# A decoder matmul over pairs of row blocks: eight half-size products become seven

## The chip, the core and the metric

The kernel runs on one core of one Trainium2 chip. The time is the device time of one execution in microseconds (us), the median of three runs. The engines are TensorE (PE in the profile, its weight loads PEld), VectorE (DVE), ScalarE (ACT), GpSimd (POOL) and the DMA queues, here that of SyncE (SP).

## What is computed

Two layers of a graph network with a normalization ahead of each, on 1250 nodes of 1024 features, 20000 edges. With `h = relu(layernorm(x))`, the first layer is

```python
h = jax.nn.sigmoid(x @ wenc.T + benc)
h2 = h @ conv_weight
msgs = h2[src] * edge_weight[:, None]
agg = jax.ops.segment_sum(msgs, dst, num_segments=x.shape[0])
hout = agg + h @ lin_weight.T
p = hout @ wdec.T + bdec
```

with 500 features inside, and `x + p` goes on. The decoder is the last line: a 1250x500 by 500x1024 product. The second layer is `x + D (A + I) D (relu(layernorm(x)) W.T + b)` with the degree scaling `D`. All of it is float32. The kernel gets float32 accuracy out of TensorE by writing each operand as a high part (rounded to fp32r or f16) and a low part, the rest; a product is then three passes: high by high, high by low, low by high.

## The kernel before

Rows come in ten blocks of 125 (`PB`), which pair up in five groups `g` of 250 (`GN`). The 500 inner features are four blocks `fo` or `j` of 125. Each engine has its own program, written out in the order in which it runs; `wait_ge` and `then_inc` on semaphores (class `Signal`) are the only ties between them. An engine does nothing ahead of an instruction that waits.

The stages in order: encoder and a count of edges into dense matrices (to about 128 us), aggregation (three steps of `AGG`; step 2, with groups 3 and 4, is the last), decoder (`decode`), second norm (`norm2_...`), the product U with the adjacency matrix (`u_group`), and the product with W (`w_product`, itself done as seven half-size products over pairs of row blocks).

**Aggregation to decoder.** ScalarE (`agg_evac`) copies each aggregated block out of PSUM as `ouhi`, VectorE subtracts to get `oulo`. The decoder weight `wd32` comes in by one 2 MB DMA, ScalarE rounds it to `wdhi`, VectorE makes `wdlo`, a quarter after each block of step 2.

**Decoder.** For each row block `k` and column half `c` TensorE does 4 feature blocks by 3 passes, 12 matmuls with 512 columns, into one of six PSUM banks (`dec_bank`): 20 tiles, 240 matmuls. A tile waits until the tile six before it has been read.

**Second norm.** For each tile VectorE adds the bank to `x1` (`residual`, the tensor that the profile shows as x) and takes its statistics; for each row block it then aggregates, ScalarE takes a root, and VectorE makes scale and bias in seven small steps (`norm2_step`) between the adds of the next block. ScalarE (`norm2_apply`) writes `ghi` (f16, 1024 wide) and two halves `t32`, a ring of four buffers; GpSimd subtracts to get `glo`, for the last block VectorE does.

**After it.** `u_group` asks for six banks at once ahead of its first matmul, 2 to 7 (`bank_of`), then goes through the row blocks `d`, twelve matmuls for each, and needs `ghi[d]` and `glo[d]`. When the last `glo` is made, SyncE loads W, and `x1` plus a bias is written away to DRAM; ScalarE's and VectorE's preparation of W (`W_hi`, `W_lo`) and GpSimd's row sums follow on that.

Of the kernel before, what the change touches and what calls it, by code (L numbers as in the profile page):

```python
# [113 lines left out]
def build(nc, x, src, dst, ew, dst_s, sd_rows, w_rows, wenc, benc, conv, lin, wdec, W, b, out):  # L114
# [331 lines left out]
    wdhi_ok = signal("wdhi_ok", one(FB))  # L446
    wdlo_ok = signal("wdlo_ok", one(FB))
# [3 lines left out]
    dec_done = signal("dec_done", KC)  # L451
    x1_ok = signal("x1_ok", KC)
    ve_ok = signal("ve_ok", one(NB))
    sqk_ok = signal("sqk_ok", one(NB))
    nb2_ok = signal("nb2_ok", one(NB))
# [1480 lines left out]
```

## Time and profile before

| | us |
|---|---|
| median of three runs | 470.31 (470.27 to 470.35) |
| profiled execution | 470.15 |
| its span in the trace | 468.3 |
| decoder on TensorE | 227.43 to 283.24 |
| TensorE busy in the span | 462.2 (99%) |
| VectorE, ScalarE, GpSimd busy | 286.6, 196.7, 109.9 |

Times inside the trace count from the start of the span. The profiled execution has 1.85 us outside its span. A busy TensorE says that a matmul was in flight; how fast they follow each other is read from the start times. Where a row of the timeline has a part in brackets, the engine stood idle before it and the bracket says for what.

### The profile page before, as it was taken

How to read it: one execution, taken by the hardware profiler on the slowest of the kernel's cores; microseconds unless marked ns; L12 is line 12 of the kernel's file. 1: busy time of each engine (PE TensorE's matmuls, PEld its weight loads, DVE VectorE, ACT ScalarE, POOL GpSimd, SP SyncE). 2: the span in 40 equal slices, each digit the busy share in tenths (PEclk: the TensorE clock that was granted, in tenths of full speed). 3: DMA queues.
4: the chain of work that ended last, by engine and by line, in shares of the span. 5: the costliest groups of instructions: out<-in, count | busy, mean ns of one | idle time of the engine just before them, and what ended most of it. 6: DMA issues, size and time to landing. Idle time of an engine off the chain costs nothing.

```text
span 468.3 us, 7228 instructions
## 1 busy us (share of the span) xinstructions
PE 462.2 (99%) x3158; PEld 369.6 (79%) x2658; DVE 286.6 (61%) x531; ACT 196.7 (42%) x371; POOL 109.9 (23%) x104
## 2 busy tenths in 40 slices
PE   8999999999999999999999999999999999999997
PEld 6999999988888899888877775444449878787876
DVE  7999878898576398022367885994130095344443
ACT  6897975855485104022024446024442512221210
POOL 2500000000040000000013443000003599895640
PEclk9999999999999999999999999999999999999999
DMA  8720004000000237100499600833310133613113
GB/s 297 272 91 2 1 2 176 2 1 1 2 1 2 83 121 247 53 0 1 173 323 174 102 1 1 316 151 131 133 69 1 57 131 145 227 55 89 44 45 91
DMA packets 26315, 44.69 MB, mean 95 GB/s; under 512 B 15525, under 2 KB 15836, under 8 KB 25638
## 3 DMA queue, kind: packets, MB, share of 16 engines
q1 hardware_dynamic: 26024, 43.77, 29.2%
q8 instruction: 25, 0.41, 0.4%
q0 software_dynamic: 224, 0.39, 0.3%
q14 instruction: 12, 0.10, 0.1%
q10 hardware_dynamic: 30, 0.02, 0.0%
HBM read 27.53 MB, written 13.41 MB: 87 GB/s over the span
## 4 chain that ended last, share of the span: by engine, by line
PE 90%; ACT 4%; DVE 4%; issue 1%; POOL 0%; POOLq 0%; DVEq 0%
PE ps L1446 87%; PE ps L1450 3%; ACT junk L718 1%; ACT zhi L747 1%; PE ps L1464 1%; ACT xn L740 1%; ACT wehi L734 1%; ACT wide L723 0%; DVE h_all L1040 0%; DVE zlo L1028 0%; ACT wide L729 0%; ACT h L756 0%; ACT h_all L759 0%; DVE h_all L1116 0%; DVE m_hot L1064 0%
## 5 line engine op out<-in xcount | busy, mean ns | idle before, releaser
L1446 PE MATMUL ps<-CT,ghi 125*128 125x500 f16 (+1 forms) x240 | 77.0, 339 | 0.0
L1446 PE MATMUL ps<-CT,glo 125*128 125x500 f16 (+1 forms) x240 | 76.9, 339 | 0.0
L1429 DVE SCALAR_TENSOR_TENSOR x1b<-ps,dsc,x1b 125x512 f32<-125x512 f32 x49 | 35.1, 746 | 34.3 <-PE ps L1446 34.2
L661 POOL TENSOR_TENSOR glo<-t,ghi 125x512 f16<-125x512 f32 x18 | 20.6, 1164 | 136.6 <-ACT t L888 136.6
L673 POOL TENSOR_TENSOR S<-U_all 128x500 f32<-128x500 f32 x25 | 31.6, 1273 | 83.8 <-DVE Blo L1403 58.6
L1446 PE MATMUL ps<-A_lo,h2hi 125*125 125x500 f32 (+1 forms) x120 | 42.3, 353 | 0.0
L1446 PE MATMUL ps<-wdhi,h_all 125*125 125x512 f32 (+1 forms) x128 | 40.3, 395 | 0.0
L1446 PE MATMUL ps<-zhi,wehi 128*125 128x250 f32 x160 | 39.3, 288 | 0.2
L1446 PE MATMUL ps<-Bhi,Shi 128*125 128x512 f32 (+1 forms) x144 | 39.3, 388 | 0.0
L1446 PE MATMUL ps<-Blo,Shi 128*125 128x512 f32 (+1 forms) x144 | 39.3, 388 | 0.0
L1446 PEld LDWEIGHTS ps<-CT,ghi 125*128 125x128 f16 x240 | 23.5, 98 | 19.0 <-issue 0.3
L1446 PEld LDWEIGHTS ps<-CT,glo 125*128 125x128 f16 x240 | 23.5, 98 | 18.8
L1446 PE MATMUL ps<-zlo,wehi 128*125 128x250 f32 x160 | 36.8, 279 | 0.0
L1446 PE MATMUL ps<-zhi,welo 128*125 128x250 f32 x160 | 36.1, 279 | 0.0
L925 ACT ACTIVATE Shi<-S 128x500 fp32r<-128x500 f32 x25 | 15.5, 622 | 47.9 <-POOL S L673 29.0
L681 POOL TENSOR_TENSOR Slo<-S,Shi 128x500 fp32r<-128x500 f32 x25 | 33.7, 1349 | 0.0
L1446 PEld LDWEIGHTS ps<-Blo,Shi 128*125 128x125 f32 x144 | 26.7, 185 | 6.4
L1446 PEld LDWEIGHTS ps<-Bhi,Shi 128*125 128x125 f32 x144 | 26.6, 185 | 6.3
L1446 PE MATMUL ps<-Ahi,h2lo 125*125 125x500 f32 x80 | 31.3, 391 | 0.0
L1446 PE MATMUL ps<-Ahi,h2hi 125*125 125x500 f32 x80 | 31.2, 390 | 0.0
L767 ACT ACTIVATE C<-ps 125x250 f16<-125x250 f32 x50 | 19.9, 398 | 26.2 <-PE ps L1450 26.1
L1446 PEld LDWEIGHTS ps<-wdhi,h_all 125*125 125x125 f32 (+1 forms) x128 | 23.8, 186 | 6.0
(181 smaller groups left out, 1032.0 us busy)
## 6 DMA issues: line engine op xcount, KB each, us to landing
xn<-in_x_dram SPq DMA_DIRECT2D x10, 512.0 KB, 5.9
x<-in_x_dram SPq DMA_DIRECT2D x10, 512.0 KB
x_scratch<-x SPq DMA_DIRECT2D x10, 500.0 KB
x1b<-x_scratch SPq DMA_DIRECT2D x10, 500.0 KB
out_dram<-x1b SPq DMA_DIRECT2D x19, 240.0 KB
B<-in_W_dram SPq DMA_DIRECT2D x4, 1024.0 KB, 8.0
c_scratch<-C SPq DMA_DIRECT2D x10, 305.2 KB
wd<-in_wdec_dram SPq DMA_DIRECT2D x1, 2048.0 KB, 15.6
```

Of the source, the lines that this page charges most:

```text
L661: p.tensor_tensor(glo[k][0:PB, cs], t32[(2 * k + c) % 4][0:PB, :], ghi[k][0:PB, cs], ALU.subtract).then_inc(*glo_p.up(k, c))
L673: p.tensor_tensor(S32[m][:, :, :], quarter(u, *one_of), quarter(u, *other), op).then_inc(*S_ok.up(u, m))
L681: p.tensor_tensor(o_ap, of, f32(Shi[W_SEQ.index((u, m)) % 6][:, :, :]), ALU.subtract).then_inc(*Slo_ok.up(u, m))
L718: a.activation(junk[0:HW], ps_all[0:HW, 0:5, 0:500], ACT.Sign, scale=-1.0, bias=thr_half[0:HW, i:i + 1], accum_out=cnt[0:HW, i:i + 1]).the ...
L734: a.activation(wehi[f][:, 0:k1, :], we32[f][:, 0:k1, :], ACT.Copy).then_inc(*whi_a.up(f, 0))
L740: a.activation(part, part, ACT.Relu, **kw).then_inc(*relu_a.up(k, h))
L747: a.activation(zhi[g % 2][:, 4 * h:4 * h + 4, i * PB:i * PB + PB], ps[turn_bank(k, h)][:, 0:4 * PB].rearrange("p (k n) -> p k n", n=PB), A ...
L767: a.activation(C[0:PB, :, u * 25:u * 25 + 25].rearrange("p a (w l) -> p a w l", w=WD), v[:, 0], ACT.Copy)
L925: a.activation(Shi[n % 6][:, :, :], of, ACT.Copy).then_inc(*Shi_ok.up(u, m))
L1429: v.scalar_tensor_tensor(r, ps[bank8["w", u, m]][0:PB, 0:512], scale, r, ALU.mult, ALU.add).then_inc(*term_ok.up(u, m, n))
L1446: return t.matmul(o_ap, lhsT, rhs, start=start, stop=stop)
L1450: return t.add_instruction(mybir.InstMatmult(name=nc.get_next_instruction_name(), engine=mybir.EngineType.PE, ins=[t.lower_ap(rhs), t.lowe ...
```

## The change

The decoder's product for a pair of row blocks is a 2 by 2 block product: two row blocks, two halves of the inner features, two halves of the columns. It was done as eight half-size products (each 2 feature blocks by 3 passes). Now it is done as seven, numbered 1 to 7, on sums and differences of blocks: `op_sums` makes four sums of the activations of a group on GpSimd (`oS`), `wd_sum` makes four sums of the weight there (`D32`), and the results of the products are added up as follows, with x11 the left half of the first row block:

- x11 += P1, P2; V = P1 + P6; V5 = V + P5; x12 += P3 + V5; x21 += V + P7 + P4; x22 += V5 + P7, where the sign of a product is in its weight's sum.

ScalarE copies P1 into `V` (`keep_product`). VectorE makes V and V5 and adds every product to `x1`, eight instructions for a pair in place of four. GpSimd adds V to x21 and V5 to x12 and x22 (`side_add`). A product takes one bank, in a ring of all eight. The activations are evacuated whole (`ou`), and high and low parts are made of blocks and sums by ScalarE (`op_hi`) and VectorE or, for groups 3 and 4, GpSimd (`op_lo`). The second norm goes by pairs. `t32` has three buffers. Four memsets at the start of VectorE's program go, since the row of ones for the bias now lies in `ohi` and GpSimd writes it.

```diff
-    wdlo = at("wdlo", RA, [128, FB, DIM], F32R)
-    wdhi = [at(f"wdhi_{j}", o, [128, DIM], F32R) for j, o in enumerate(
-        [RA + 16384 + j * 4096 for j in range(3)] + [RH + 4 * H_SLOT])]
...
+    ou = [at(f"ou_{g}", RH + g * H_SLOT, [128, FB, GN], F32) for g in range(NG)]
+    oulo = [at(f"oulo_{g}", RH + g * H_SLOT, [128, FB, GN], F32R) for g in range(NG)]
+    oS = [at(f"oS_{g}", RH + g * H_SLOT + 4000, [128, 4, 2, PB], F32) for g in range(NG)]
+    oSlo = [at(f"oSlo_{g}", RH + g * H_SLOT + 4000, [128, 4, 2, PB], F32R) for g in range(NG)]
+    ohi = [at(f"ohi_{g}", RG + g * 8192, [128, 7, 2, PB], F32R) for g in range(NG)]
+    V = [at(f"V_{i}", RA + 40960 + i * 2048, [128, 512], F32) for i in range(2)]
+    V5 = [at(f"V5_{i}", RA + 45056 + i * 2048, [128, 512], F32) for i in range(2)]
...
-    t32 = [at(f"t32_{i}", t32o[i], [128, 512], F32) for i in range(4)]
+    t32 = [at(f"t32_{i}", RH + i * 2048, [128, 512], F32) for i in range(3)]
...
+    D_ORDER = (1, 6, 2, 5, 3, 7, 4)
+    D_OP = {1: 0, 2: 1, 4: 2, 5: 3, 6: 4, 7: 5, 3: 6}
+    D_BANKS = (7, 0, 1, 6, 2, 3, 4, 5)
+    D_READ = {1: "x11a", 6: "V", 2: "x11b", 5: "V5", 3: "x12", 7: "x22", 4: "x21b"}
...
+        def op_sums(g):
+            A11, A12, A21, A22 = (ou[g][0:PB, 2 * j:2 * j + 2, i * PB:i * PB + PB] for i in range(2) for j in range(2))
+            S1, S2, S3, S4 = (oS[g][0:PB, i] for i in range(4))
+            p.wait_ge(*ou_ok.at(g, FB - 1))
+            p.tensor_tensor(S1, A21, A22, ALU.add).then_inc(*ps_step.up())
+            first = ps_step.now()
+            p.tensor_tensor(S3, A11, A21, ALU.subtract)
+            p.wait_ge(*first)
+            p.tensor_tensor(S2, S1, A11, ALU.subtract).then_inc(*ps_step.up())
+            p.wait_ge(*ps_step.now())
+            p.tensor_tensor(S4, A12, S2, ALU.subtract).then_inc(*oS_ok.up(g))
...
+        op_sums(0)
+        op_sums(1)
+        p.wait_ge(*agg_done.at(1, FB - 1))
+        op_ones(0)
+        p.wait_ge(*d_wd.at())
+        B11, B12, B21, B22 = (wd32[:, i] for i in range(4))
+        wd_sum(7, B22, B12)
+        p.wait_ge(*dsum_ok.at(7))
+        wd_sum(5, B12, B11)
+        p.wait_ge(*dsum_ok.at(5))
+        wd_sum(6, B22, D32[5])
+        p.wait_ge(*dsum_ok.at(6))
+        wd_sum(4, B21, D32[6])
+        op_sums(2)
+        p.wait_ge(*agg_done.at(2, 0))
+        op_ones(1)
+        op_ones(2)
+        p.wait_ge(*agg_done.at(2, FB - 1))
+        op_ones(3)
+        op_ones(4)
+        wd_lo(5)
+        def side_add(g, what, of, after):
+            k, c = 2 * g + int(what[1]) - 1, int(what[2]) - 1
+            r = x1[0:PB, k, 512 * c:512 * c + 512]
+            p.wait_ge(*add_ok.at(g, after))
+            if what == "x21":
+                p.wait_ge(*d_x1[k].at("x"))
+            p.tensor_tensor(r, r, of[g % 2][0:PB, :], ALU.add).then_inc(*side_ok.up(g, what))
+        for g in range(NG):
+            side_add(g, "x21", V, "V")
+            if g < 2:
+                op_sums(g + 3)
+            else:
+                gather_lo((0, 2, 4)[g - 2])
+            side_add(g, "x12", V5, "x12")
+            side_add(g, "x22", V5, "x22")
+            if g < 2:
+                for i in range(3):
+                    op_lo(g + 3, i)
+            elif g < NG - 1:
+                gather_lo((1, 3)[g - 2])
+        for k in range(5, NB - 1):
+            gather_lo(k)
...
+        def op_hi(g):
+            a.wait_ge(*ones_ok.at(g))
+            a.wait_ge(*oS_ok.at(g))
+            for i in range(3):
+                a.activation(op_high(g, i), op_of(g, i), ACT.Copy).then_inc(*ohi_ok.up(g, i))
+        def keep_product(g):
+            if g >= 2:
+                a.wait_ge(*side_ok.at(g - 2, "x21"))
+                a.wait_ge(*add_ok.at(g - 2, "V5"))
+            a.wait_ge(*dec_done.at(g, 1))
+            a.activation(V[g % 2][0:PB, :], ps[dec_bank(g, 1)][0:PB, 0:512], ACT.Copy).then_inc(*kept_ok.up(g))
...
+            if (step, fo) == (2, FB - 1):
+                a.wait_ge(*agg_done.at(step, fo))
+                wd_hi(5)
+                wd_hi(3)
+                keep_product(0)
+                wd_hi(7)
+                wd_hi(4)
...
+        op_hi(3)
+        keep_product(1)
+        for g in range(NG):
+            norm2_root(g)
+            if g == 0:
+                op_hi(4)
+            norm2_apply(2 * g)
+            if g + 2 < NG:
+                keep_product(g + 2)
+            norm2_apply(2 * g + 1)
...
-        for g in range(NG - 1):
-            v.memset(f32(hhi[g][:, 0, :]), 1.0).then_inc(*one_row.up(g))
...
+        def norm2_step(g, n):
+            ks = slice(2 * g, 2 * g + 2)
+            each = [slice(k, k + 1) for k in range(2 * g, 2 * g + 2)]
+            y, t, s2, var, dg = (col[name] for name in ("ry", "rt", "sc2", "ve", "nb"))
             if n == 0:
-                v.wait_ge(*sqk_ok.at(k))
-                v.reciprocal(y, col["sq"][0:PB, ks]).then_inc(*vs.up())
+                v.wait_ge(*sqk_ok.at(g))
+                v.reciprocal(y[0:PB, ks], col["sq"][0:PB, ks]).then_inc(*vs.up())
             else:
                 v.wait_ge(*step_done[0])
             if n == 1:
-                v.tensor_tensor(t, y, y, ALU.mult).then_inc(*vs.up())
+                for k in each:
+                    v.tensor_scalar(t[0:PB, k], y[0:PB, k], var[0:PB, k], y[0:PB, k], ALU.mult, ALU.mult).then_inc(*vs.up())
             if n == 2:
-                v.tensor_tensor(t2, t, var, ALU.mult).then_inc(*vs.up())
+                v.tensor_scalar(t[0:PB, ks], t[0:PB, ks], -0.5, 1.5, ALU.mult, ALU.add).then_inc(*vs.up())
             if n == 3:
-                v.tensor_scalar(t, t2, -0.5, 1.5, ALU.mult, ALU.add).then_inc(*vs.up())
+                for k in each:
+                    v.tensor_scalar(s2[0:PB, k], t[0:PB, k], y[0:PB, k], dg[0:PB, k], ALU.mult, ALU.mult).then_inc(*vs.up())
             if n == 4:
-                v.tensor_tensor(r, t, y, ALU.mult).then_inc(*vs.up())
-            if n == 5:
-                v.tensor_scalar(s2, r, col["dinv"][0:PB, ks], GSCALE, ALU.mult, ALU.mult).then_inc(*vs.up())
-            if n == 6:
-                v.scalar_tensor_tensor(col["nb2"][0:PB, ks], mv[0:PB, k, 0:1], -1.0, s2, ALU.mult, ALU.mult
-                                       ).then_inc(*nb2_ok.up(k))
+                for i, k in enumerate(each):
+                    ins = v.tensor_scalar(col["nb2"][0:PB, k], mv[0:PB, 2 * g + i, 0:1], s2[0:PB, k], -1.0, ALU.mult, ALU.mult)
+                ins.then_inc(*nb2_ok.up(g))
             step_done[0] = vs.now()
...
+        for g in range(NG):
+            if g == 0:
+                wd_lo(3)
+            else:
+                norm2_stats(g - 1, 1, 0)
+                norm2_stats(g - 1, 0, 1)
+            shared_sum(g)
+            add_product(g, 1, "x11a")
+            add_product(g, 2, "x11b")
+            if g == 0:
+                wd_lo(7)
+            else:
+                norm2_stats(g - 1, 1, 1).then_inc(*vs.up())
+                step_done[0] = vs.now()
+            right_sum(g)
+            if g == 0:
+                wd_lo(4)
+            else:
+                norm2_var(g - 1)
+            norm2_stats(g, 0, 0)
+            add_product(g, 3, "x12")
+            for n in range(2 if g else 0):
+                norm2_step(g - 1, n)
+            add_product(g, 7, "x21a")
+            for n in range(2, 4 if g else 2):
+                norm2_step(g - 1, n)
+            add_product(g, 7, "x22")
+            for n in range(4, 5 if g else 4):
+                norm2_step(g - 1, n)
+            add_product(g, 4, "x21b")
...
+                    if n >= 8:
+                        g0, i0 = divmod(n - 8, 7)
+                        t.wait_ge(*add_ok.at(g0, D_READ[D_ORDER[i0]]))
+                    elif n == 0:
+                        t.wait_ge(*ou_ok.at(2, FB - 1))
+                    elif n in (4, 7):
+                        t.wait_ge(*ou_ok.at(NG - 1, FB - 2 if n == 4 else FB - 1))
+                    o_ap = ps[dec_bank(g, m)][0:PB, 0:512]
+                    op, i = D_OP[m], op_part(m)
+                    q0, i0 = (0 if op == 0 else 2), (PB if op == 2 else 0)
+                    t.wait_ge(*ohi_ok.at(g, i))
+                    if g == 0:
+                        t.wait_ge(*dhi_ok.at(m))
+                    for j in range(2):
+                        K = PB + 1 if m in (1, 5) and j == 0 else PB
+                        mm(o_ap, ohi[g][0:K, op, j, :], Dhi[m][0:K, j, :], j == 0, False)
+                    t.wait_ge(*(olo_v if g < 3 else olo_p).at(g, i))
+                    for j in range(2):
+                        L = oulo[g][0:PB, q0 + j, i0:i0 + PB] if op < 3 else oSlo[g][0:PB, op - 3, j, :]
+                        mm(o_ap, L, Dhi[m][0:PB, j, :], False, False)
+                    if g == 0:
+                        t.wait_ge(*(dlo_v if (m,) in dlo_v.values else dlo_p).at(m))
+                    for j in range(2):
+                        K = PB + 1 if m in (1, 5) and j == 0 else PB
+                        ins = mm(o_ap, ohi[g][0:K, op, j, :], Dlo[m][0:K, j, :], False, j == 1)
+                    ins.then_inc(*dec_done.up(g, m))
...
-                if bank < 6:
-                    t.wait_ge(*x1_ok.at(*KC[18 + bank if bank < 2 else 12 + bank]))
+                g0, i0 = divmod(max(n for n in range(7 * NG) if D_BANKS[n % 8] == bank), 7)
+                t.wait_ge(*add_ok.at(g0, D_READ[D_ORDER[i0]]))
```

**VectorE, one pair of row blocks in the decoder, before** (second norm of one block `k`, done twice for a pair; x_156 is `x1`, rt, sc_68 and nb_69 are small columns):

```order
L1328 TENSOR_TENSOR x_156<-x_156,ps 125x512
L1340 RECIPROCAL ry<-sq 125x1
L1328 TENSOR_TENSOR x_156<-x_156,ps 125x512
L1344 TENSOR_TENSOR rt<-ry 125x1
L1332 BN_STATS stats<-x_156 125x6
L1346 TENSOR_TENSOR rt_65<-rt,ve 125x1
L1332 BN_STATS stats<-x_156 125x6
L1348 TENSOR_SCALAR rt<-rt_65 125x1
L1350 TENSOR_TENSOR rstd<-rt,ry 125x1
L1352 TENSOR_SCALAR sc_68<-rstd,dinv 125x1
L1354 SCALAR_TENSOR_TENSOR nb_69<-mv,sc_68 125x1
L1375 BN_AGGR mv<-stats 125x2
```

**and after** (one pair; x_195 is `x1`, V_173 is V, V_0_175 is V5):

```order
L1492 TENSOR_TENSOR V_173<-V_173,ps 125x512
L1486 TENSOR_TENSOR x_195<-x_195,ps 125x512 x2
L1508 BN_STATS stats<-x_195 125x6
L1501 TENSOR_TENSOR V_0_175<-V_173,ps 125x512
L1512 BN_AGGR mv<-stats 125x2
L1513 BN_AGGR mv<-stats 125x2
L1128 TENSOR_SCALAR ve<-mv 125x2
L1508 BN_STATS stats<-x_195 125x6
L1486 TENSOR_TENSOR x_195<-x_195,ps 125x512
L1524 RECIPROCAL ry<-sq 125x2
L1529 TENSOR_SCALAR rt<-ry,ve 125x1 x2
L1486 TENSOR_TENSOR x_195<-x_195,ps 125x512
```

The four adds and four statistics of a pair have become eight adds or sums and four statistics, and the small instructions run once for a pair on two columns or two after each other.

**ScalarE, from the end of the aggregation to the second pair's norm, after** (ohi are the high parts of a group's activations, V_173 and V_174 the kept products, ghi and t the norm's outputs):

```order
L964 ACTIVATE ohi_171<-ou_151 125x500
L964 ACTIVATE ohi_171<-ou_151 125x250
L964 ACTIVATE ohi_171<-oS_161 125x1000
L972 ACTIVATE V_174<-ps 125x512
L1019 ACTIVATE sq<-ve 125x2
L964 ACTIVATE ohi_172<-ou_152 125x500
L964 ACTIVATE ohi_172<-ou_152 125x250
L964 ACTIVATE ohi_172<-oS_162 125x1000
L1024 ACTIVATE ghi_196<-x_195,nb_69,sc_68 125x1024
L1029 ACTIVATE t_0_217<-x_195,nb_69,sc_68 125x512
L1029 ACTIVATE t_1_218<-x_195,nb_69,sc_68 125x512
L972 ACTIVATE V_173<-ps 125x512
```

The copies of product 1 (L972) stand in the row with the norm's writes; before, nothing but roots and those writes stood here.

**GpSimd, over the same stretch, after** (L698 to L704 are the sums of a group, L756 the side adds, L712 low parts):

```order
L719 TENSOR_TENSOR Dlo_182<-wd_177,Dhi_191 126x1024
L756 TENSOR_TENSOR x_195<-x_195,V_173 125x512
L698 TENSOR_TENSOR oS_161<-ou_151 125x250
L700 TENSOR_TENSOR oS_161<-ou_151 125x250
L702 TENSOR_TENSOR oS_161<-oS_161,ou_151 125x250
L704 TENSOR_TENSOR oS_161<-ou_151,oS_161 125x250
L756 TENSOR_TENSOR x_195<-x_195,V_0_175 125x512 x2
L712 TENSOR_TENSOR oulo_156<-ou_151,ohi_171 125x4x125
L712 TENSOR_TENSOR oulo_156<-ou_151,ohi_171 125x2x125
L712 TENSOR_TENSOR oSlo_166<-oS_161,ohi_171 125x1000
L756 TENSOR_TENSOR x_195<-x_195,V_174 125x512
L698 TENSOR_TENSOR oS_162<-ou_152 125x250
```

Before, only the subtractions for `glo` stood here. The sums and low parts of groups 3 and 4 now stand between the side adds of groups 0 and 1.

## Rows read from the trace of the kernel before

**Rows 1.** the page: busy time, share of the span, instructions; then the chain

```profile
PE 462.2 (99%) x3158; PEld 369.6 (79%) x2658; DVE 286.6 (61%) x531; ACT 196.7 (42%) x371; POOL 109.9 (23%) x104
...
PE 90%; ACT 4%; DVE 4%; issue 1%; POOL 0%; POOLq 0%; DVEq 0%
```

**Rows 2.** the busy time by stretch: decoder, then U's first half

```profile
core 0: us, PE busy (x) PEld busy (x) DVE busy (x) ACT busy (x) POOL busy (x), PEclk, DMA share, GB/s
...
227.40:283.20 55.80, 55.80 (x241) 44.37 (x239) 39.92 (x116) 21.51 (x34) 16.05 (x14) 1.00 0.73 162
...
283.20:317.00 33.80, 33.80 (x162) 15.68 (x162) 29.76 (x36) 9.87 (x16) 4.54 (x4) 1.00 0.42 165
```

**Rows 3.** TensorE's timeline: start, duration (us), matmul (decoder begins, U begins)

```profile
227.43 0.39 PE L1446 MATMUL ps<-wdhi,ouhi 126*125 126x512 f32 x1
...
283.24 0.38 PE L1446 MATMUL ps<-CT,ghi 125*128 125x500 f16 x1
```

**Rows 4.** VectorE's timeline in the decoder

```profile
241.78 0.69 DVE L1328 TENSOR_TENSOR x<-x,ps 125x512 f32<-125x512 f32 x1
...
242.39 0.15 DVE L1340 RECIPROCAL ry<-sq 125x1 f32<-125x1 f32 x1
...
247.45 0.16 DVE L1354 SCALAR_TENSOR_TENSOR nb<-mv,sc 125x1 f32<-125x1 f32 x1
...
247.53 0.20 DVE L1375 BATCH_NORM_AGGREGATE mv<-stats 125x2 f32<-125x12 f32 x1
...
247.76 0.15 DVE L982 TENSOR_SCALAR ve<-mv 125x1 f32<-125x1 f32 x1
```

**Rows 5.** groups of instructions: count, busy us, mean ns of one, idle before

```profile
L1296 DVE TENSOR_TENSOR wdlo<-wd,wdhi 128x1024 fp32r<-128x1024 f32 x4 | 4.8, 1224 | 0.6 <-ACT wdhi L876 0.6
...
L884 ACT ACTIVATE ghi<-x,nb,sc 125x1024 f16<-125x1024 f32 x10 | 12.3, 1227 | 0.0
...
L888 ACT ACTIVATE t<-x,nb,sc 125x512 f32<-125x512 f32 x20 | 15.1, 802 | 0.0
...
L925 ACT ACTIVATE Shi<-S 128x500 fp32r<-128x500 f32 x25 | 15.5, 622 | 47.9 <-POOL S L673 29.0
...
L876 ACT ACTIVATE wdhi<-wd 128x1024 fp32r<-128x1024 f32 x4 | 4.1, 1060 | 0.0
...
L661 POOL TENSOR_TENSOR glo<-t,ghi 125x512 f16<-125x512 f32 x18 | 20.6, 1164 | 136.6 <-ACT t L888 136.6
...
L673 POOL TENSOR_TENSOR S<-U_all 128x500 f32<-128x500 f32 x25 | 31.6, 1273 | 83.8 <-DVE Blo L1403 58.6
...
L681 POOL TENSOR_TENSOR Slo<-S,Shi 128x500 fp32r<-128x500 f32 x25 | 33.7, 1349 | 0.0
```

**Rows 6.** the timeline where VectorE and GpSimd want SBUF together

```profile
249.98 0.69 DVE L1328 TENSOR_TENSOR x<-x,ps 125x512 f32<-125x512 f32 x1 [1.37 <-PE ps L1446]
...
250.08 2.29 POOL L661 TENSOR_TENSOR glo<-t,ghi 125x512 f16<-125x512 f32 x2 [3.77 <-ACT t L888]
...
251.79 0.60 DVE L1346 TENSOR_TENSOR rt<-rt,ve 125x1 f32<-125x1 f32 x1
...
17.13 0.99 POOL L625 DMA_INDIRECT sdw<-in_sd_rows_dram,row_i  x1 [0.30 <-issue]
...
17.75 0.35 DVE L1000 TENSOR_SCALAR ry<-ve 125x2 int32<-125x2 int32 x1
```

**Rows 7.** the page's DMA issues: KB, us to landing

```profile
wd<-in_wdec_dram SPq DMA_DIRECT2D x1, 2048.0 KB, 15.6
```

**Rows 8.** VectorE's timeline at the start: the four memsets

```profile
2.16 1.07 DVE L1116 MEMSET h_all<- 128x250 f32 x4
```

**Rows 9.** the timeline behind the decoder: VectorE, GpSimd and TensorE

```profile
293.77 12.04 DVE L1393 SCALAR_TENSOR_TENSOR x<-bb,vb,x 125x1024 f32<-125x1024 f32 x10
...
350.84 2.46 POOL L673 TENSOR_TENSOR S<-U_all 128x500 f32<-128x500 f32 x2 [58.60 <-DVE Blo L1403]
...
367.70 1.16 PE L1446 MATMUL ps<-Bhi,Shi 128*125 128x512 f32 x4
```

More of the change, by code:

```diff
@@ L437, in build @@
     OU_PARTS = [(g, fo) for gs in AGGS for fo in range(FB) for g in gs]
-    ouhi_ok = signal("ouhi_ok", OU_PARTS)
-    oulo_ok = signal("oulo_ok", OU_PARTS)
+    ou_ok = signal("ou_ok", OU_PARTS)
+    oS_ok = signal("oS_ok", one(NG))
+    ones_ok = signal("ones_ok", one(NG))
+    OP_PARTS = [(g, i) for g in range(NG) for i in range(3)]
+    ohi_ok = signal("ohi_ok", OP_PARTS)
+    olo_v = signal("olo_v", OP_PARTS[:9])
+    olo_p = signal("olo_p", OP_PARTS[9:])
+    ps_step = Steps(sem("pool_step"))
     deg_a = signal("deg_a", [(k,) for k in range(0, NB, 2)])
@@ L445, in build @@
     va_ok = signal("va_ok", one(NB))
[L446 to L455, printed above, removed]
+    dsum_ok = signal("dsum_ok", [(7,), (5,), (6,), (4,)])
+    dhi_ok = signal("dhi_ok", [(1,), (2,), (6,), (5,), (3,), (7,), (4,)])
+    dlo_v = signal("dlo_v", [(1,), (2,), (6,), (3,), (7,), (4,)])
+    dlo_p = signal("dlo_p", [(5,)])
+    GM = [(g, m) for g in range(NG) for m in D_ORDER]
+    dec_done = signal("dec_done", GM)
+    add_ok = signal("add_ok", [(g, what) for g in range(NG) for what in ("V", "x11a", "x11b", "V5", "x12", "x21a", "x22", "x21b")])
+    kept_ok = signal("kept_ok", one(NG))
+    side_ok = signal("side_ok", [(g, what) for g in range(NG) for what in ("x21", "x12", "x22")])
+    ve_ok = signal("ve_ok", one(NG))
+    sqk_ok = signal("sqk_ok", one(NG))
+    nb2_ok = signal("nb2_ok", one(NG))
     ghi_ok = signal("ghi_ok", one(NB))
@@ L1280, in vector @@
         for step, fo, groups, parts in AGG:
-            for n in groups:
-                agg_evac(n, fo)
             for part in parts:
                 split_A(*part)
+            if (step, fo) == (1, FB - 1):
+                v.wait_ge(*dsum_ok.at(5))
+                wd_lo(1)
+                v.wait_ge(*dsum_ok.at(4))
+                wd_lo(2)
+                op_lo(0)
+            if step == 2 and fo < 2:
+                if fo == 0:
+                    wd_lo(6)
+                op_lo(fo + 1)
             if step == 0:
@@ new lines, in norm2_stats, with norm2_var @@
+        def norm2_stats(g, half, c):
+            k = 2 * g + half
+            v.wait_ge(*{(0, 0): add_ok.at(g, "x11b"), (1, 0): add_ok.at(g, "x21b"), (0, 1): side_ok.at(g, "x12"),
+                        (1, 1): side_ok.at(g, "x22")}[half, c])
+            return v.bn_stats(stats[0:PB, k, c, :], x1[0:PB, k, 512 * c:512 * c + 512])
+        def norm2_var(g):
+            v.wait_ge(*step_done[0])
+            v.bn_aggr(mv[0:PB, 2 * g, :], stats[0:PB, 2 * g].rearrange("p a s -> p (a s)"))
+            v.bn_aggr(mv[0:PB, 2 * g + 1, :], stats[0:PB, 2 * g + 1].rearrange("p a s -> p (a s)")).then_inc(*vs.up())
+            v.wait_ge(*vs.now())
+            with_eps(2 * g, 2 * g + 2).then_inc(*ve_ok.up(g))
@@ L1378, in vector, with late_stats @@
-        for n in range(7):
-            norm2_step(NB - 1, n)
+        def late_stats(g):
+            norm2_stats(g, 1, 0)
+            norm2_stats(g, 0, 1)
+            norm2_stats(g, 1, 1).then_inc(*vs.up())
+            step_done[0] = vs.now()
[10 more added lines that the diff above has]
+                wd_lo(7)
+            else:
+                norm2_stats(g - 1, 1, 1).then_inc(*vs.up())
+                step_done[0] = vs.now()
+            right_sum(g)
+            if g == 0:
+                wd_lo(4)
+            else:
+                norm2_var(g - 1)
[10 more added lines that the diff above has]
+            add_product(g, 4, "x21b")
@@ L1380, in vector @@
+        late_stats(NG - 1)
+        norm2_var(NG - 1)
+        for n in range(5):
+            norm2_step(NG - 1, n)
         k = NB - 1
```

190 lines of the change are left out of this document (95 added, 95 removed).

## The prediction

> **What bounds the kernel now.** First the page's busy line and its chain [rows 1]: TensorE is busy 99% of the span and the chain that ended last is 90% TensorE, so a microsecond of matmuls taken out is a microsecond won, unless a wait takes its place. Then the stages [rows 2]: in the decoder and in U after it TensorE never stops, at a granted clock of 1.00 (2.4 GHz), while VectorE is busy 39.9 of 55.8 us, ScalarE 21.5, GpSimd 16.1. Those three get the new work. Then TensorE's start times [rows 3]: 240 matmuls from 227.43 to 283.24 are 55.81 us, 0.2325 us each (the duration of 0.39 overlaps the next one).
>
> **TensorE's part.** 7 products x 5 groups x 6 matmuls = 210, of the same 512 columns and the same three passes. 30 fewer x 0.2325 = **6.98 us less**; a group takes 42 x 0.2325 = 9.77 us in place of 11.16, all five 48.8, and the decoder could end at 276.3. Nothing is added on TensorE.
>
> **Prices for the rest.** VectorE starts the instruction behind a 512-wide add 0.61 us later (241.78 to 242.39 [rows 4]); small ones follow each other in 0.08 us when independent and 0.23 when one waits for the other (247.45, 247.53, 247.76 [rows 4]). The two-pointer `tensor_scalar` of the new norm has no row; between 0.08 and 0.25 I take 0.13, since they come in independent pairs. A 1024-wide subtraction on VectorE is 1.22, taken as 1.17 back to back [rows 5]. ScalarE [rows 5], less 0.1 us that neighbours overlap: `ghi` 1.13, a `t` 0.71, a copy of 500 elements 0.52, of 250 half of that and a little, 0.28, of 1024 0.96. The copy of product 1 has the size of the 500-element one, about 0.60 to its end. GpSimd: 1.16 to 1.35 us for 500 to 512 elements [rows 5], 1.23 apart in the two at 350.84 [rows 9], so 1.25 for a side add, 1.14 for half a `glo`, about 0.65 for 250 elements, 2.4 for 1000. A handover between engines is 0.05 to 0.15.
>
> **The port.** A VectorE instruction with two SBUF inputs that needs 0.14 lasts 0.60 while GpSimd works (251.79 plus 0.60 is 252.39, GpSimd ends at 252.37 [rows 6]): it waits until GpSimd's instruction is over. An add from PSUM keeps its 0.69 beside GpSimd (249.98 [rows 6]). A two-column `tensor_scalar` lasts 0.35, where small ones take 0.15 to 0.20 [rows 4], and ends as GpSimd's descriptor write does, at 18.1 [rows 6].
>
> **What the edits cost ahead of the decoder.** The weight's and activations' sums and the high and low parts for groups 0 to 2 are covered by TensorE's step 2, 168 matmuls of 500 columns or some 38 us, in which the other engines mostly wait for it. The weight lands 15.6 us after its issue [rows 7]; even if that were issued only as step 2 starts, GpSimd's four weight sums, 9.6 us, and one group's, 2.6 us, would end 10 us ahead of the decoder. So they cost nothing; without that cover they would cost those 12 us. At 227.45 it gets tight. ScalarE rounds weight 5 (to 228.5), GpSimd makes its low part, 2.4 us, to 231.0, and VectorE, which wanted weight 3 at 229.5, is held off the port until then: V(0) is done at 232.9. Weights 7 and 4 come just late for TensorE, together about 0.6 us, so its own end is **276.9**.
>
> **The chain through V.** Three things stand in a row that before had nothing to do with each other. Product 1 must be copied by ScalarE before VectorE can make V; ScalarE's copy for group g+2 stands behind `norm2_apply(2g)`; that waits for the norm of group g, whose last small step VectorE takes near the end of its work for group g+1.
>
> Start of it: GpSimd's side add ends at 234.1. VectorE's low parts of weights 7 and 4 take the port (1.17 each) between the sums of group 3, which end at 239.1. Two side adds to 241.6; low parts of group 3, 1.23 + 0.62 + 2.40, to 245.8; side add to 247.1; sums of group 4, 4 x 0.65 and 0.2 of port, to 249.9. ScalarE's high parts of group 4, 0.52 + 0.28 + 0.95, stand ahead of the first norm writes: 251.7; `ghi` and two `t`, 1.13 + 1.42: 254.2; the copy and handover: **V(2) starts at 254.9**. TensorE had product 6 of group 2 ready at about 250.5.
>
> A lap, V(g) to V(g+1): on VectorE nine wide instructions (V, two adds, statistics, V5, statistics, three adds) 9 x 0.61 = 5.5; one of them waits for its neighbour, 0.1; small ones 1.6 (2 aggregates and epsilon 0.41, reciprocal 0.19, three pairs 0.78, one of two columns 0.18): 7.2, with 0.1 for the root that is late once. On ScalarE handover 0.1, `ghi` 1.13, `t` 0.71, a wait of 0.35 (the ring has three buffers, and the one needed is freed by GpSimd only after the side add of x22, 1.25, and half a `glo`, 1.14), `t` 0.71, copy and handover 0.65: 3.65. Together 10.95, and about 0.25 for the two-column step held by the port: **11.2 us, where TensorE needs 9.77**.
>
> Two laps: V(4) starts at 277.3. TensorE does not feel it inside the decoder, since eight banks let it run seven products (9.8 us) ahead. It feels it at the end: U asks for banks 2 to 7 before its first matmul, and bank 7 holds the last group's product 3, whose add (x12) VectorE starts 5 x 0.61 + 0.1 + 0.4 + 0.61 = 4.2 us after V(4), at 281.5, and ends at 282.2. So TensorE stands from 276.9 to 282.3, **5.4 us**, and U begins at 282.3 in place of 283.24. Of 6.98 us, 0.9 are left.
>
> **The rest.** The four memsets, 1.07 us [rows 8], leave VectorE's start. Behind them stands the cast that TensorE and ScalarE wait for, so between 0 and 1.07; VectorE then waits for the x rows' DMA anyway, so I take 0.2. After the decoder: the last `glo`, made 16 us after x12 (rest of the adds and statistics, norm steps, then ScalarE's six writes, paced by GpSimd's halves of 1.14), comes at about 298.4, and VectorE's bias (293.77 [rows 9]), the loads of W and GpSimd's first sums (350.84 [rows 9]) move some 4.6 us later, to 355.5; these sums and their low parts take 4.9 us, to 360.4, and TensorE wants them at 367.7 [rows 9] less 1.1. Covered, and covered for `glo[d]` too: U takes 2.5 us for a block. Sum: 470.15 of the profiled execution less 0.9 less 0.2 = 469.05; the median lies 0.16 above that execution, so **469.2**.
>
> **A rule against the trace.** The row of the held instruction and the row of the two-column one [rows 6] are all that this trace shows of the port. The Trainium skill ("SBUF — State Buffer", section "SBUF: two separate sides") says that VectorE's two-input instructions and those in a two-port mode share one exclusive port pair with GpSimd, for the whole instruction. The trace agrees for two inputs. By that rule the epsilon step (two columns, one input) would be held as well, which is rival B: 471.0 where the sum above has 469.2.
>
> **Rivals.**
> - A, the lag stays small. If GpSimd's 250-wide sums and the pairs on VectorE are quicker, V(2) starts at 252.5 and the lap is 10.5 without port and ring waits: x12 at 277.7 to 278.4, U at 278.5, gain 4.7, 465.4; if the lap is below 9.8 the change does all it says, 463.3. For it: the port waits are short where GpSimd idles. Against: the order of ScalarE's program is fixed, and nine adds of 0.61 are measured. 463 to 468, chance 0.20.
> - B, slower: small steps held by the port. GpSimd works 5 x 1.2 us of each lap, so each held step costs up to 1.25. With epsilon held too a lap is 12.1: V(4) 279.1, U at 284.1, 471.0. With all pairs held a lap is 13.1: U at 286.1, 473.0. The point from which the change loses: lap = 11.2 + 0.95 / 2 = 11.7. Chance 0.20.
> - C, slower: the clock. TensorE is idle 5.4 us in one piece, longer than any gap in this trace, where the granted clock is 1.00 [rows 2]. If it drops to 1.2 GHz for as long as the gap was, U's matmuls go at half rate for 5.4 us: 2.7 lost, 471.9. The Trainium skill ("TensorE: Matmul & The Clock Gate", section "Part 1: The HAM clock gate (the "warmup" mystery)") says that idleness throttles the array to that level; no row here shows it. Chance 0.15.
> - The forecast, U between 280.8 and 283.8, 467.7 to 470.8: 0.40. Something else, mostly at the start or in the W stage: 0.05.
>
> **How the numbers follow.** The range leaves out the best tenth (below 466.0, most of A's lower half) and the tail of B: 466.0 to 473.0. A measurement of this kernel tells 0.2% (0.94 us) from no change, so faster ends at 469.4. Faster: 0.27 of the forecast's 0.40, all of A, 0.01 of the rest: 0.48. Same (to 471.25): 0.12 + 0.08 of B + 0.02 of C + 0.02: 0.24. Slower: 0.01 + 0.12 + 0.13 + 0.02: 0.28.
>
> **What would show it.** TensorE without a gap in the decoder but with one of 4 to 6 us between its last matmul and the first of U, put down to VectorE's add into x (L1486). V's adds (L1492) near 254.9, 266.1 and 277.3. VectorE idle before each of them for ScalarE's copy (L972). I am wrong if that gap is under 3 us or the V's are less than 10.5 apart (A), if the two-column steps last over 0.5 (B), or if the granted clock of the first 10 us of U is under 0.9 (C).

## The result, and the profile after

The changed kernel takes 472.18 us (median of five, 471.38 to 472.87), the kernel before 470.28 (470.27 to 470.35) in the same comparison: ratio 1.0041, 95% interval 1.0029 to 1.0052. It is slower by 1.9 us, where 469.2 was forecast. The profiled execution took 472.11 and has a span of 470.1.

TensorE's busy line, the clock by fortieths of the span, and the chain, from the page of the changed kernel (of before: [rows 1]):

```profile
PE 458.6 (98%) x3128; PEld 365.0 (78%) x2628; DVE 296.4 (63%) x504; ACT 210.9 (45%) x389; POOL 172.2 (37%) x159
PEclk9999999999999999999999997999999999999999
PE 85%; DVE 6%; POOL 3%; issue 3%; ACT 2%; DMA 1%; DVEq 0%; POOLq 0%; ACTq 0%
```

Thirty matmuls are gone, the chain's share on TensorE fell from 90% to 85%, and one slice of the clock, the 25th (282 to 294 us), is not full. TensorE's longest wait behind 46 us (engine, line, what for: us in all, times, longest; the only other, 0.4 us, lies ahead of the decoder), and its timeline around the decoder's end:

```profile
PE ps L1649 <- DVE x L1486: 5.8, 1, 5.8
```

```profile
276.18 0.63 PE L1649 MATMUL ps<-Dlo,ohi 125*125 125x512 f32 x2
282.64 0.58 PE L1649 MATMUL ps<-CT,ghi 125*128 125x500 f16 x1 [5.83 <-DVE x L1486]
283.01 0.62 PE L1649 MATMUL ps<-CT,glo 125*128 125x500 f16 x1
283.42 0.63 PE L1649 MATMUL ps<-CT,ghi 125*128 125x500 f16 x1
...
287.18 0.51 PE L1649 MATMUL ps<-CT,glo 125*128 125x500 f16 x1
287.52 0.38 PE L1649 MATMUL ps<-CT,ghi 125*128 125x500 f16 x1
287.73 0.37 PE L1649 MATMUL ps<-CT,glo 125*128 125x500 f16 x1
```

The decoder is over at 276.65 (276.18 and two starts of 0.2325), U begins at 282.64, where it was 283.24 [rows 3]: one wait, for the add of the last group's product 3 (x12). The profile calls it 5.8 us; counted from the slot in which the next matmul would have started it is 6.0. Then U's first twelve matmuls start 0.42 us apart, the later ones 0.211. The same by stretch (start:end, us, TensorE busy, granted clock, DMA share, GB/s):

```profile
276.00:282.60 6.60, 0.81 (x4) 0.85 0.00 0
282.60:287.60 5.00, 4.96 (x13) 0.52 0.02 5
287.60:292.60 5.00, 5.00 (x26) 1.00 0.00 0
```

After the wait the granted clock is 0.52, the level of 1.2 GHz, and TensorE, busy all the time, gets 13 matmuls into 5 us in place of 26. The level fell inside the wait already, where the mean is 0.85. From 282.64 to 287.52 there are twelve matmuls, 4.88 us; at 0.211 they would be 2.53. That is **2.35 us lost**, and the whole account is: start of the decoder 227.14 for 227.43, 0.3 less; 30 matmuls, 7.0 less; waits inside the decoder, 0.7 more; the wait at its end, 6.0 more; the clock, 2.35 more. Sum +1.8, as the span says (470.1 less 468.3).

What the wait hangs on, on VectorE, ScalarE and GpSimd (V of groups 2, 3 and 4, and what is ahead of them):

```profile
253.92 0.69 DVE L1492 TENSOR_TENSOR V<-V,ps 125x512 f32<-125x512 f32 x1 [3.03 <-ACT V L972]
257.34 0.17 DVE L1128 TENSOR_SCALAR ve<-mv 125x2 f32<-125x2 f32 x1
265.05 0.69 DVE L1492 TENSOR_TENSOR V<-V,ps 125x512 f32<-125x512 f32 x1 [1.71 <-ACT V L972]
268.47 0.92 DVE L1128 TENSOR_SCALAR ve<-mv 125x2 f32<-125x2 f32 x1
272.97 0.33 DVE L1537 TENSOR_SCALAR nb<-mv,sc 125x1 f32<-125x1 f32 x2
276.92 0.69 DVE L1492 TENSOR_TENSOR V<-V,ps 125x512 f32<-125x512 f32 x1 [1.71 <-ACT V L972]
280.35 0.86 DVE L1128 TENSOR_SCALAR ve<-mv 125x2 f32<-125x2 f32 x1
281.72 0.66 DVE L1486 TENSOR_TENSOR x<-x,ps 125x512 f32<-125x512 f32 x1
```

```profile
273.33 1.24 ACT L1024 ACTIVATE ghi<-x,nb,sc 125x1024 f16<-125x1024 f32 x1 [3.71 <-DVE nb L1537]
274.48 0.80 ACT L1029 ACTIVATE t<-x,nb,sc 125x512 f32<-125x512 f32 x1
275.59 0.82 ACT L1029 ACTIVATE t<-x,nb,sc 125x512 f32<-125x512 f32 x1 [0.31 <-POOL glo L725]
276.31 0.57 ACT L972 ACTIVATE V<-ps 125x512 f32<-125x512 f32 x1
```

```profile
267.07 2.28 POOL L725 TENSOR_TENSOR glo<-t,ghi 125x512 f16<-125x512 f32 x2
278.91 2.27 POOL L725 TENSOR_TENSOR glo<-t,ghi 125x512 f16<-125x512 f32 x2
```

The rows read as a loop: VectorE's last norm step of group 2 (272.97) lets ScalarE write `ghi` and two `t`, only then comes the copy of product 1 of group 4 (276.31), and VectorE, idle for 1.71 us, starts V(4) at 276.92. A lap, from one V to the next, is 11.13 and then 11.87 us. In the second the epsilon step of two columns (it adds the norm's small constant to the variances of two row blocks) takes 0.92 and ends at 269.39, when GpSimd's pair does (269.35); the same at 280.35, on the way to x12.

### The profile page after: what moved, and what is told of

Read it like the earlier page. It is cut to its first block, busy times and chain, and to the rows that moved or that the text cites. A ratio compares the mean times of both kernels' runs of the same rounds, so it can differ in the third digit from the quotient of the medians.

```text
span 470.1 us, 7278 instructions
## 1 busy us (share of the span) xinstructions
PE 458.6 (98%) x3128; PEld 365.0 (78%) x2628; DVE 296.4 (63%) x504; ACT 210.9 (45%) x389; POOL 172.2 (37%) x159
## 4 chain that ended last, share of the span: by engine, by line
PE 85%; DVE 6%; POOL 3%; issue 3%; ACT 2%; DMA 1%; DVEq 0%; POOLq 0%; ACTq 0%
PE ps L1649 80%; PE ps L1653 3%; DVE x L1486 2%; PE ps L1667 1%; POOL x L756 1%; DVE stats L1508 1%; DMA xn<-in_x_dram 1%; ACT ohi L964 1%; POOL wehi L671 1%; DVE V L1501 1%; POOL glo L725 0%; ACT V L972 0%; DVE xn L1270 0%; POOL oS L698 0%; POOL oS L700 0%
## 5 line engine op out<-in xcount | busy, mean ns | idle before, releaser
L1649 PE MATMUL ps<-CT,ghi 125*128 125x500 f16 (+1 forms) x240 | 78.4, 345 | 5.8 <-DVE x L1486 5.8
L1649 PE MATMUL ps<-CT,glo 125*128 125x500 f16 (+1 forms) x240 | 78.3, 345 | 0.0
L691 POOL TENSOR_TENSOR C<-C,loops 125x125 f16<-125x125 f16 x10 | 3.7, 405 | 110.1 <-DVE got L1389 110.1
L958 ACT ACTIVATE ou<-ps 125x250 f32<-125x250 f32 x20 | 6.7, 377 | 49.3 <-PE ps L1649 49.3
L1649 PE MATMUL ps<-Bhi,Slo 128*125 128x512 f32 (+1 forms) x104 | 28.4, 385 | 0.0
```

Of the source, the lines that this page charges most:

```text
L958: a.activation(ou[g][0:PB, fo, :], agg_put(g, fo), ACT.Copy).then_inc(*ou_ok.up(g, fo))
L1649: return t.matmul(o_ap, lhsT, rhs, start=start, stop=stop)
```

## Experiments

Spans and rows are of the profiled executions; V(2), V(3) and V(4) are the starts of VectorE's V of these groups.

**Filling the idle stretch**, to get the clock's price apart from the wait.

```diff
+            for i in range(26):
+                mm(ps[6][0:PB, 0:500], identh[0:PB, 0:PB], CT[0:PB, 0, 0:500], i == 0, i == 25)
```

> The changed kernel with 26 matmuls of 500 columns (about 5.5 us at full clock) put between the decoder's last matmul and U's first one. They write a bank that is free by then and that U overwrites; nothing of the computation changes. The wait of U for bank 7 stays. Theory (the idle stretch of TensorE lowers the granted clock, and that is worth 2.4 us): U begins at 282.6 as before, its first twelve matmuls stand 0.211 us apart in place of 0.417, the clock stays at 1.00, total 469.8. Rival (U's first matmuls are slow for another reason, such as glo or CT being read beside the other engines' work, not for the idle stretch): they stay at 0.417 apart and the total stays at 472.1.

The span fell to 467.9 (all ten executions 467.8 to 468.1, clock 0.999 to 1.000), TensorE's timeline:

```profile
276.56 5.65 PE L1649 MATMUL ps<-CT,identh 125*125 125x500 f16 x26
282.65 0.37 PE L1649 MATMUL ps<-CT,ghi 125*128 125x500 f16 x1 [0.45 <-DVE x L1486]
282.86 0.37 PE L1649 MATMUL ps<-CT,glo 125*128 125x500 f16 x1
283.07 0.37 PE L1649 MATMUL ps<-CT,ghi 125*128 125x500 f16 x1
```

U begins at the same time and its matmuls are 0.21 apart. So it is the idle stretch that makes them slow, and it costs 2.2 us of span. In time it is 1.5 us (470.66 for 472.18). The median total, 470.66 (ratio 1.0010, 1.0000 to 1.0020), is 0.9 above the 469.8 expected. In this kernel the total stood some 2.8 us above the span, in the other changed kernels about 2.0, in the kernel before 1.8. Nothing in the trace shows why; this stays open.

**Taking the copy out of the loop.**

```diff
-            norm2_apply(2 * g)
             if g + 2 < NG:
                 keep_product(g + 2)
+            norm2_apply(2 * g)
             norm2_apply(2 * g + 1)
```

> The changed kernel with ScalarE's copy of product 1 of group g+2 moved ahead of both norm writes of group g. Theory (the chain through V: V(g+2) waits for a copy that stands behind the norm of group g): V(2) starts near 251.4, V(3) near 260.8, V(4) near 270.2; bank 7 is free at 275.7, before TensorE's own end at 276.7, so U begins at 276.7 without a gap and without a drop of the clock; total 463.8. Rival (VectorE's own work in a group, with the waits for the port, is what takes more than TensorE's 9.8 us): laps stay near 11, V(4) later than 273, U begins after 279, total above 468.

465.27 us, ratio 0.9893 (0.9877 to 0.9910). V(2) came at 251.52, VectorE's waits for the copy fell from 6.4 to 0.5 us, U began at 278.31 at full clock. So the loop was the cause, and moving one call turns the loss into a gain of 5 us (the clock's 2.2 included). But V(3) was at 263.19 and V(4) at 272.90, not 260.8 and 270.2, and a wait of 1.4 us was left. VectorE and ScalarE show why:

```profile
258.59 0.17 DVE L1524 RECIPROCAL ry<-sq 125x2 f32<-125x2 f32 x1 [2.14 <-ACT sq L1019]
```

```profile
257.65 0.81 ACT L1029 ACTIVATE t<-x,nb,sc 125x512 f32<-125x512 f32 x1 [1.77 <-POOL glo L725]
258.37 0.19 ACT L1019 ACTIVATE sq<-ve 125x2 f32<-125x2 f32 x1
```

ScalarE's root for the next norm stood behind a `t` that waited for GpSimd. In the changed kernel VectorE was never early enough to feel it.

**The two-column steps.**

```diff
-            with_eps(2 * g, 2 * g + 2).then_inc(*ve_ok.up(g))
+            with_eps(2 * g, 2 * g + 1)
+            with_eps(2 * g + 1, 2 * g + 2).then_inc(*ve_ok.up(g))
```

and the step `1.5 - 0.5 t` in the same way.

> The changed kernel with the two two-column steps of the norm (epsilon and 1.5 - 0.5 t) written as two one-column instructions each. Theory (a two-column tensor_scalar is held until GpSimd's instruction ends, a one-column one is not): the epsilon step that lasted 0.92 and 0.86 us takes 0.25 for the pair, V(4) starts 0.7 us earlier, U begins near 281.2, the clock drops as before, total 470.8. Rival (what holds it is not the width, but a wait for the aggregate or the port for every instruction of this kind): durations up to 0.9 us remain, U begins near 282.6, total 472.1.

```profile
268.55 0.21 DVE L1128 TENSOR_SCALAR ve<-mv 125x1 f32<-125x1 f32 x2
```

Beside the same GpSimd work the pair takes 0.21 where one two-column instruction took 0.92. V(4) was at 276.18, 0.74 earlier, U began at 281.26. In this step the width decides. The total was 470.04 (ratio 1.0001, 0.9991 to 1.0011), 0.8 better than expected, since the clock cost less in most executions: six of ten have a mean clock of 0.996 and spans of 467.7 to 468.1, four have 0.993 and 468.7 to 469.3.

**Asking for bank 7 late.**

```diff
-                    banks = {k: bank_of(("u", p, k)) for k in ks}
+                    late = 5 if 5 in ks else None
+                    banks = {k: bank_of(("u", p, k)) for k in ks if k != late}
...
+                            banks[late] = bank_of(("u", p, late))
```

> The changed kernel with U's first pass asking for bank 7 only after the first three row blocks have been put into the other five banks; the same matmuls in another order. Theory (U waits for the add that reads the last group's product 3 in bank 7): U now waits for product 5 in bank 5, whose add ends at 280.1, and begins at 280.2, 2.4 us earlier, after an idle stretch of 3.5 us. If that lowers the clock as the one of 5.8 us did, the total is 469.7; if it does not, 467.3. Rival (U's start is set by something else, such as ghi, glo or CT): U still begins at 282.6, total 472.1.

```profile
280.70 0.58 PE L1649 MATMUL ps<-CT,ghi 125*128 125x500 f16 x1 [3.62 <-DVE V L1501]
...
283.15 0.61 PE L1649 MATMUL ps<-CT,ghi 125*128 125x500 f16 x1
283.57 0.41 PE L1649 MATMUL ps<-CT,glo 125*128 125x500 f16 x1
283.81 0.37 PE L1649 MATMUL ps<-CT,ghi 125*128 125x500 f16 x1
```

U now waits for V5, as said, and begins 1.9 us earlier (2.4 were expected); seven matmuls are slow, 1.4 us. 469.28 us, ratio 0.9980 (0.9971 to 0.9990). So it was bank 7 that held U.

**The root ahead of the last norm write**, on top of the copy first.

```diff
+                if c == 1 and root is not None:
+                    norm2_root(root)
                 if n >= 3:
                     a.wait_ge(*glo_p.at(*KC[n - 3]))
```

> The copy of product 1 first, as in e2_keep_first, and besides ScalarE's root for the norm of group g+1 ahead of the last norm write of group g. In e2_keep_first VectorE stood 2.14 us at 256.4 for that root, because the write ahead of it waited for GpSimd. Theory (that wait was what kept V(4) at 272.9 and left a gap of 1.4 us): V(3) near 261.1, V(4) near 270.8, product 3 of the last group added by 276.0, U begins at TensorE's own end, 276.8, without a gap; total 463.8. Rival (VectorE's own lap of 9.7 us and the port take it back, or the norm writes now come too late for U): V(4) later than 272 or a new wait inside U, total 464.8 or more.

Median 464.25, ratio 0.9871 (0.9855 to 0.9888). Three executions took 464.2, near what the theory gives; the profiled one 465.50, and it shows V(3) at 260.95, as expected, but V(4) at 272.92. Between them:

```profile
264.36 2.81 DVE L1129 TENSOR_SCALAR ve<-mv 125x2 f32<-125x2 f32 x1
```

```profile
263.61 1.29 POOL L756 TENSOR_TENSOR x<-x,V 125x512 f32<-125x512 f32 x1
264.85 2.29 POOL L725 TENSOR_TENSOR glo<-t,ghi 125x512 f16<-125x512 f32 x2
```

A step that needs 0.17 ended at 267.17, with the last of three GpSimd instructions that followed each other without a pause (267.14), not with the one that was running when it came (264.90). It isn't always so: in the same execution the step at 276.32 ended at 276.88, inside a row of two of GpSimd's.

```profile
276.32 0.56 DVE L1129 TENSOR_SCALAR ve<-mv 125x2 f32<-125x2 f32 x1
```

**e5_root with one-column pairs** takes the wait away:

> e6_all without its change to the order of VectorE's low parts of weights 7 and 4: so e5_root with the two-column steps of the norm as one-column pairs. In the profiled execution of e5_root the two-column epsilon step of group 2 lasted 2.81 us beside three GpSimd instructions in a row, U began at 278.3 and the total was 465.50, where its other executions took 464.2. Theory (that step was held by GpSimd, and one-column steps are not): all executions near 464.2, no step of the norm over 0.3 us, U begins at TensorE's own end 276.8. The difference to e6_all is then the 0.5 us of the two weights. Rival (the long step has another cause): some executions stay near 465.5.

463.77 us, ratio 0.9862 (0.9846 to 0.9879), spans 461.5 to 461.8, no epsilon step over 0.22 for the pair, U at 276.55 without a wait. That is 0.4 less than the 464.2 expected.

**All of it, with VectorE's low parts of weights 7 and 4 one step earlier:**

```diff
             shared_sum(g)
+            if g == 0:
+                wd_lo(7)
             add_product(g, 1, "x11a")
             add_product(g, 2, "x11b")
             if g == 0:
-                wd_lo(7)
+                wd_lo(4)
```

> e5_root with two more edits: the two-column steps of the norm as one-column pairs, and VectorE's low parts of weights 7 and 4 each one step earlier, ahead of the two adds of product 1 and 2 of group 0, and ahead of its V5. Theory (TensorE's 0.7 us of waits in group 0 are those two low parts): TensorE's own end moves from 276.8 to 276.3 and U begins there; total 463.3. Rival (TensorE's waits in group 0 come from another operand, or the low parts are held by GpSimd in their new places): TensorE's end stays at 276.8, total 463.8.

```profile
235.01 1.70 DVE L1405 TENSOR_TENSOR Dlo<-D,Dhi 126x1024 fp32r<-126x1024 f32 x1
...
275.88 0.63 PE L1652 MATMUL ps<-Dlo,ohi 125*125 125x512 f32 x2
276.35 0.39 PE L1652 MATMUL ps<-CT,ghi 125*128 125x500 f16 x1
276.57 0.37 PE L1652 MATMUL ps<-CT,glo 125*128 125x500 f16 x1
```

463.64 us, ratio **0.9860 (0.9843 to 0.9876)**, the best here: 6.6 us under the kernel before. The laps are 9.28 and 9.26 us, under TensorE's 9.77. The last edit did less than expected: weight 7 is no longer late, but weight 4 still is, since its low part, at its new place beside GpSimd's sums, takes 1.70 us where it took 1.21. So the rival holds in part: U begins 0.2 earlier than without the edit, and the two medians can't be told apart.

**The memsets back.** The four memsets and ScalarE's wait for them, as they were.

> The changed kernel with VectorE's four memsets at the start of the span put back, at their old place, and ScalarE's wait for them. By the prediction they are worth 0.2 us of the start (between 0 and 1.07); by the two traces, where the first decoder matmul starts at 227.43 with them and at 227.14 without, 0.3. Expected: the first transposes of the d rows start at 3.54 in place of 3.24, the first decoder matmul at 227.4, total 472.4. Rival (the 0.3 is scatter between two executions): both times stay, total 472.1.

```profile
3.54 2.34 PE L1654 MATMUL ps<-d,identh 5*126 5x500 f16 x5 [0.35 <-DVE d L1267]
```

The first transposes are at 3.54 again, as in both profiles of the old kernel, and at 3.12 to 3.43 in the nine profiles without memsets. The decoder begins at 227.59 here (227.43 and 227.59 in the old kernel), without memsets between 227.07 and 227.40. So the memsets are worth some 0.3, with a scatter of 0.2 from one execution to the next. The total, 473.34 for one execution, holds 14 slow matmuls (2.9 us) and says no more.

**An idle stretch in the kernel before.** SyncE, after the decoder's last matmul:

```diff
+        for i in range(3):
+            q.dma_start(benc_t[0:PB, :], benc).then_inc(*d_gap.up(i))
+            q.wait_ge(*d_gap.at(i))
```

> The kernel before with an idle stretch put between the decoder and U: when the decoder's last matmul is done, SyncE reads a small tile three times, one transfer after the other, and TensorE waits for the last; nothing of the computation changes. Theory (an idle stretch of 5 to 6 us lowers the granted clock, whatever kernel it is in): about 6 us idle, then twelve or so matmuls 0.417 us apart in place of 0.211, so the span grows by the stretch and 2.4 us more, to about 476.7 (total 478.5). Rival (the drop belongs to the changed kernel's other load on the chip): the clock stays at 1.00 and the span grows by the stretch alone.

```profile
288.14 0.39 PE L1450 MATMUL ps<-CT,ghi 125*128 125x500 f16 x1 [4.59 <-DMA benc_t<-in_benc_dram]
288.37 0.44 PE L1450 MATMUL ps<-CT,glo 125*128 125x500 f16 x1
288.60 0.62 PE L1450 MATMUL ps<-CT,ghi 125*128 125x500 f16 x1
...
291.51 0.60 PE L1450 MATMUL ps<-CT,glo 125*128 125x500 f16 x1
291.93 0.39 PE L1450 MATMUL ps<-CT,ghi 125*128 125x500 f16 x1
```

The stretch was shorter than planned, 4.6 us. Two matmuls ran at full speed, then eight at half: 1.7 us. The granted clock is 1.00 from 283.5 to 288.1 and 0.50 from 288.6 to 291.9. The span grew by 6.7, of which U's start (4.9 later) and the slow matmuls are 6.6. The old kernel, with its other load on the engines, behaves in the same way in this one execution, so the rival falls.

**Half the filling.** `e1_fill` with 13 matmuls.

> e1_fill with 13 of its 26 matmuls: TensorE works until 279.4 and is then idle for about 3.2 us before U's first matmul at 282.6. In e4_late_bank an idle stretch of 3.6 us was followed by seven matmuls at half rate (1.4 us), in e3_eps_split one of 4.3 us by seven or twelve (1.4 or 2.4 us). Theory (the price of the idle stretch grows with its length and is not a fixed 2.4 us): zero to seven slow matmuls, span 467.9 to 469.2. Rival (any idle stretch before U costs the full 2.4 us): twelve slow matmuls, span 470.1. It also tells whether the total stands 2.0 us above the span, as in the other kernels, or 2.8, as it did in e1_fill.

```profile
276.33 2.91 PE L1649 MATMUL ps<-CT,identh 125*125 125x500 f16 x13
282.33 0.37 PE L1649 MATMUL ps<-CT,ghi 125*128 125x500 f16 x1 [3.09 <-DVE x L1486]
282.54 0.37 PE L1649 MATMUL ps<-CT,glo 125*128 125x500 f16 x1
...
283.52 0.62 PE L1649 MATMUL ps<-CT,glo 125*128 125x500 f16 x1
```

471.27 us, from 469.63 to 472.60: spans of 467.6 once, 469.1 to 469.4 four times, 470.6 once. Their mean clocks are 1.000, 0.996 and 0.993 in the same order. So one and the same program, with a stretch of 3.1 us in the profiled execution, lost nothing, about 1.6 or 3.0 us to the clock from one execution to the next. The theory put the upper end at 469.2 and one execution passed it; the rival's fixed price falls. The totals stood 2.0 above the spans here.

The stretches side by side:

| kernel | idle ahead of U, us | slow matmuls, cost in us (profiled execution) |
|---|---|---|
| e1_fill | 0.45 | 0 |
| e5_root, e2_keep_first | 1.3, 1.4 | 0 |
| e9_fill_half | 3.1 | 9, 1.7 |
| e4_late_bank | 3.6 | 7, 1.4 |
| e3_eps_split | 4.3 | 13, 2.55 |
| e8_before_gap | 4.6 | 8, 1.7 |
| changed kernel | 5.8 | 12, 2.35 |
| e7_memsets | 5.8 | 14, 2.9 |

## Why the forecast was wrong

**The step that failed** is the clock in the sum. The prediction let U run at full speed after 5.4 us of idle time, since no row of before had such a stretch, and kept the drop as rival C with a chance of 0.15 and 471.9 us. The drop came in all five executions (mean clock 0.993 in each). Of the 3.1 us between the 469.05 of the sum and the 472.11 of the profiled execution the clock is 2.35. U's start is 0.5 (282.64, where the sum has 282.3 less the 0.2 of the memsets), and the last 0.15 stands outside the span (2.0 for 1.85). Without the clock's part the change would have been 0.4 us faster than before, so the clock decided the sign, not the whole miss. C's time missed the measured one by 0.3. C's way of pricing, half the stretch (2.7), was of the right size for no good reason: the cost did not follow the length (table). The Trainium skill ("TensorE: Matmul & The Clock Gate", section "Part 1: The HAM clock gate (the "warmup" mystery)") says that an idle array goes to 1.2 GHz; the trace agrees, with 0.52 granted after 5.8 us. The prediction cites the same section and still gave C 0.15. It had no row against the drop, and with C the likelier case the forecast would have been a loss.

**The rest, by its steps.**

- TensorE's 210 matmuls and its own end: 276.9 forecast, 276.65 measured. The waits for weights 7 and 4, 0.6, were 0.7.
- V(2): 254.9, measured 253.92. The order on GpSimd and ScalarE was right. GpSimd's work was priced too long: the low parts of group 3 took 3.7 us (241.31 to 245.00) for 4.25, the sums of groups 3 and 4 together 0.5 less than counted.
- The lap: 11.2, measured 11.13 and 11.87. The forecast let one two-column step wait 0.25; the epsilon step waited 0.75 in the second lap and 0.7 once more before x12. So B's mechanism was there in part. Its full price, 12.1 a lap, was not reached, because in the first lap the step took 0.17 (257.34). It came in the middle of a row of two GpSimd instructions (256.29 to 258.60), most likely between them. B's own sum left out that the same step stands on the way to x12 too.
- x12 over at 282.2 and U at 282.3: measured 282.38 and 282.64. Two errors, 1.0 down in V(2) and 1.2 up in the laps and on the way to x12, cancelled. That these two times came out is luck.
- That U's start hangs on bank 7 was shown by e4_late_bank, the loop through ScalarE by e2_keep_first.
- The memsets, 0.2: the runs say about 0.3.
- Behind the decoder: GpSimd's first sums at 355.5, measured 355.40 (before 350.84 [rows 9]), the product with W 1.75 later than before, as U is, with no wait. Covered as said.
- A's condition, a lap of 10.5 or less, was not met by the change as it stands. e10_no_lo and e6_all reach a lap under 9.8 (9.26 to 9.33), and take 463.77 and 463.64. A's 463.3 left out the 0.6 for the two weights and the 0.2 of the memsets. With both it would have been 463.8.

The seven products were worth what the matmul count says. The order on ScalarE took it away, and the clock turned the rest into a loss.

## To carry to other kernels

Where an in-order engine gets a new small job that another engine waits for, place it ahead of the long ones that are in nobody's way: here one call moved by a place was worth 6.9 us of 472. A wait of some microseconds on TensorE is to be priced above its length: nothing more at 1.3 and 1.4 us, up to 2.9 us more at 5.8, and from nothing to 3.0 at 3.1. One that can't be removed may be filled with idle matmuls into a free bank, which gave back 1.5 us of time here. When the bound of a stretch moves to VectorE, look at its small steps beside GpSimd, not only at its wide ones.

## What the hardware showed that was not expected

- The price of an idle stretch of TensorE varies from one execution to the next (0, 1.6 or 3.0 us of span for 3.1 us of idle time), and the fall to the lower level can come after the work has begun again: two matmuls into U in e8_before_gap, four in e9_fill_half. The changed kernel's five spans spread over 1.5 us, where with the stretch filled all ten lie within 0.3, so this is most likely the clock too.
- A two-column `tensor_scalar` with one SBUF input and immediate scalars waits for GpSimd (0.92 for 0.17), two one-column ones don't (0.21 for both), and the wait can outlast the instruction that was running: 2.81 us over three in a row, seen once. The Trainium skill ("SBUF — State Buffer", section "SBUF: two separate sides") says that the loser is blocked for the whole instruction of the other; the run shows that it can be more than one.
